# A scan that keeps fourteen state chunks in a ring and reads a whole step out at once

## The reference, cut to what matters

```
h = layernorm(patches of x) @ W + bias, layernorm      # 32 images, 14 x 14 patches -> 196 tokens of 256
h = concatenate([h, txt])                              # 77 text tokens more: 273 tokens
# attention stand-in: every second token goes through a gated recurrence
x_sub = rmsnorm(layernorm(h)[:, ::2]); x, gate = split(x_sub @ w_in.T + b_in)
for each of the 137 steps:                             # state: 32 batches x 256 x 64
    state = tanh(state * A + x_t[:, :, None] * Bm)
    y_t   = state @ c_sum + Dv * x_t
h = h + repeat((y * silu(gate)) @ w_out.T + b_out, 2)
h = h + down(silu(gate(ln(h))) * up(ln(h)))            # integer weights, hidden size 768
```

## Time and profile before

| | |
|---|---|
| median of three runs | 1458.93 us |
| profiled execution | 1453.06 us |
| its span | 1451.3 us |
| PE (matmul) busy | 1244.6 us (86%) |
| DVE busy | 1076.0 us (74%) |
| ACT busy | 1005.0 us (69%) |
| POOL busy | 483.4 us (33%) |
| mean granted TensorE clock | 0.957 of full speed |

### The profile page before, as it was taken

The page is one execution under the profiler, slowest core; times in us unless marked ns, Lnnn a source line. Parts: engine busy times, 40 slices in busy tenths (PEclk is TensorE's granted clock), DMA queues, the critical chain, the costliest instruction groups (busy, mean ns, idle before and its releaser), DMA issues.

```text
span 1451.3 us, 25794 instructions
## 1 busy us (share of the span) xinstructions
PE 1244.6 (86%) x7119; PEld 636.8 (44%) x7119; DVE 1076.0 (74%) x2401; ACT 1005.0 (69%) x1955; POOL 483.4 (33%) x463
## 2 busy tenths in 40 slices
PE   3777889898998989999999999998888989879855
PEld 1642445454544444445445544544344334333333
DVE  4667878787878697878687878776877878768721
ACT  1367686868776868686868786866866867758622
POOL 5213151525343434433334343432222131221231
PEclk9789999999999999999999999999999999999987
DMA  6221414132232314141404050303132231222110
GB/s 180 64 65 32 96 46 96 52 88 72 67 84 55 89 51 102 37 111 28 116 23 120 20 126 13 103 18 101 43 88 75 65 88 50 74 62 63 52 51 7
DMA packets 154925, 100.50 MB, mean 69 GB/s; under 512 B 129088, under 2 KB 143296, under 8 KB 153536
## 3 DMA queue, kind: packets, MB, share of 16 engines
q1 hardware_dynamic: 154880, 99.95, 27.3%
HBM read 58.85 MB, written 41.06 MB: 69 GB/s over the span
## 4 chain that ended last, share of the span: by engine, by line
PE 42%; ACT 21%; issue 11%; DVE 9%; DMA 8%; SPq 4%; POOL 2%; ACTq 1%; DVEq 0%; POOLq 0%
PE P L1179 9%; PE Y L1135 9%; ACT h L883 9%; PE U L1125 8%; DMA raw<-in_x 6%; DVE U L695 5%; PE P L1269 4%; PE P L1270 4%; PE P L1224 3%; ACT rawn L894 2%; PE P L1210 2%; ACT xT_act L967 2%; ACT xT_act L900 2%; ACT fsg L963 2%; ACT y_fx L950 1%
## 5 line engine op out<-in xcount | busy, mean ns | idle before, releaser
L695 DVE TENSOR_TENSOR U<-h,a_col 128x512 f32<-128x512 f32 x1096 | 726.1, 690 | 199.2 <-ACT h L883 193.0
L883 ACT ACTIVATE h<-U 128x512 f32<-128x512 f32 x1096 | 627.2, 601 | 293.1 <-PE U L1125 290.2
L1125 PE MATMUL U<-x_diag,b_st 128*128 128x512 f16 x1096 | 395.7, 392 | 120.7 <-DVE U L695 110.2
L1135 PE MATMUL Y<-h,read_st 128*32 128x512 f32 x2192 | 300.3, 621 | 0.7 <-ACT h L883 0.7
L1125 PEld LDWEIGHTS U<-x_diag,b_st 128*128 128x128 f16 x1096 | 105.8, 100 | 385.4 <-DVE U L695 290.2
L1065 POOL TENSOR_TENSOR xT_act<-act,xT_act 128x448 f16<-128x448 f32 x120 | 123.0, 1038 | 209.3 <-ACT xT_act L967 209.3
L1179 PE MATMUL P<-tok_w,xT_act 128*112 128x256 f32 x672 | 167.8, 385 | 0.9 <-ACT xT_act L900 0.9
L1179 PEld LDWEIGHTS P<-tok_w,xT_act 128*112 128x112 f32 x672 | 118.8, 179 | 40.2 <-issue 11.2
L1284 PE MATMUL P<-down_w,xT_act 128*112 128x256 bf16 x480 | 116.6, 279 | 4.9 <-POOL xT_act L1065 4.9
L1285 PE MATMUL P<-down_w,xT_act 128*112 128x256 bf16 x480 | 115.4, 277 | 0.0
L1019 POOL TENSOR_TENSOR yT<-yT,gate_fx 128x448 f32<-128x448 f32 x20 | 22.7, 1133 | 272.2 <-DMA yT<-y_scr 272.2
(11 more groups left out here) (135 smaller groups left out, 1466.6 us busy)
## 6 DMA issues: line engine op xcount, KB each, us to landing
raw<-in_x SPq DMA_DIRECT2D x42, 448.0 KB, 6.1
tok_scr<-tok SPq DMA_DIRECT2D x20, 448.0 KB, 3.3
gate_scr<-gate_o SPq DMA_DIRECT2D x20, 448.0 KB, 2.5
gate_fx<-gate_scr SPq DMA_DIRECT2D x20, 448.0 KB, 5.0
res<-tok_scr SPq DMA_DIRECT2D x20, 448.0 KB, 3.7
out<-res SPq DMA_DIRECT2D x76, 112.0 KB, 2.3
x_diag<-scan_scr SPq DMA_DIRECT2D x320, 16.0 KB
x_diag<-scan_scr SPq DMA_DIRECT2D x304, 12.0 KB
```

The lines of the kernel that those rows point to most:

```text
L695: dve.tensor_tensor(U[bank_of(slot)][:, :].rearrange("p (l b) -> p l b", b=B), h[:, c, :].rearrange("p (l b) -> p l b", b=B), a_col[:, c * ...
L883: sc.activation(h[:, c, :], U[bank_of(slot)][:, :], ACT.Tanh, scale=1.0 / U_SCALE).then_inc(squashed, 1)
L1125: pe.matmul(U[bank_of(slot)][:, :], b_st[:, c, :], x_diag[:, c, :, t * B:t * B + B], start=False, stop=True, skip_group_check=True).then_i ...
L1135: mm = pe.matmul(Y[c4 * 32:c4 * 32 + 32, :], read_st[:, t, half, :], h[:, half * RG + c4, :], start=(j == 0), stop=(t == steps - 1), skip_ ...
```

## The change

The tile `h` gets 14 places instead of 8 and is used as a ring: slot n writes place n mod 14, and `grow` of slot n reads place (n-8) mod 14. 56 slots are four rounds of the ring, so the numbering goes on through the bodies. The old state of a chunk now lives until 14 slots later. `read_group` becomes `read_step`: eight matmuls for one step, behind the drive of slot 8t+11 (and, for a scan's last step, behind the drive of slot 3 of the next body). On SP the load of yT moves ahead of the text loads. All tables have other numbers. `h` is cleared at the start over its new length; the program is built with a smaller scratch area for software-made DMA descriptors (`dynamic_dma_scratch_size=8192`), and it issues no DMA from POOL.

```diff
-READ_AT = 2
+READ_AT = 3
+RING = 14
...
     "text": dict(
-        ... attend=(13, 17) ... finish=(10, 12) ... ln_stats=(11,), ln_shift=(15,), ... y_copy=(2,)
+        ... attend=(19, 20) ... finish=(15, 17) ... ln_stats=(20,), ln_shift=(21,), ... y_copy=(3,)
...
-        h = sb("h", [128, CHUNKS, CW])
+        h = sb("h", [128, RING, CW])
...
+            if post:
+                sp.wait_ge(y_wr, (q + 1) * 64)
+                sp.sem_inc(passed, 1)
+                for d2 in range(2):
+                    sp.dma_start(yT[d2:127 + d2:2, :, :, :]..., y_scr[:, :, :, d2, :]...).then_inc(y_ld, 16)
             if pre and not image:
...                                                      # the text loads
-            if post:
-                sp.wait_ge(y_wr, (q + 1) * 64)
-                ...                                      # the same two loads of yT
...
-                                  h[:, c, :].rearrange("p (l b) -> p l b", b=B),
+                                  h[:, (slot - CHUNKS) % RING, :].rearrange("p (l b) -> p l b", b=B),
...
-                sc.activation(h[:, c, :], U[bank_of(slot)][:, :], ACT.Tanh, scale=1.0 / U_SCALE)...
+                sc.activation(h[:, slot % RING, :], U[bank_of(slot)][:, :], ACT.Tanh, scale=1.0 / U_SCALE)...
...
-            def read_group(j, s, steps):
-                t, half = divmod(j, 2)
-                pe.wait_ge(squashed, s * SLOTS + (j + 1) * RG)
-                if j == 0 and due(s):
+            def read_step(t, s, steps):
+                pe.wait_ge(squashed, s * SLOTS + (t + 1) * CHUNKS)
+                if t == 0 and due(s):
                     pe.wait_ge(y_out, s)
-                for c4 in range(RG):
-                    mm = pe.matmul(Y[c4 * 32:c4 * 32 + 32, :], read_st[:, t, half, :], h[:, half * RG + c4, :], ...)
+                for half in range(CHUNKS // RG):
+                    for c4 in range(RG):
+                        mm = pe.matmul(Y[c4 * 32:c4 * 32 + 32, :], read_st[:, t, half, :],
+                                       h[:, (t * CHUNKS + half * RG + c4) % RING, :], ...)
...
-                    if slot % RG == READ_AT and slot >= RG:
-                        read_group(slot // RG - 1, s, steps)
+                    if slot % CHUNKS == READ_AT and slot >= CHUNKS:
+                        read_step(slot // CHUNKS - 1, s, steps)
                     elif slot == READ_AT and due(s):
-                        read_group(SLOTS // RG - 1, s - 1, STEPS)
+                        read_step(STEPS - 1, s - 1, STEPS)
```

More of the change, by code:

```diff
@@ L63 @@
     "image": dict(
[L64 to L72, removed]
+        shrink=(0, 0, 0, 2, 5, 5, 6, 7), turn=(9, 9, 10, 11, 15, 15, 16, 16), attend=(17, 18), average=(22, 26),
@@ L77 @@
-        res_stats=(24,), res_variance=(26,), res_shift=(28,), fx_low_part=(35, 35), ln_stats=(11,), ln_shift=(15,),
-        x_low_part=(38,), ffn_product=(40, 44, 45, 49, 53, 55), y_copy=(2,), fx_apply=(27, 27, 28, 29),
-        fxT_copy=(31, 32), ln_apply=(14,), xaT_copy=(17,), x_copy=(24,), gate_silu=(41,), ffn_silu=(36, 38, 40, 46,
-        48, 53), act_high_part=(48, 50, 53, 54, 55, 55)),
+        shrink=(6, 7, 8, 8, 13, 13, 14, 16), attend=(19, 20), turn_fx=(33, 33), ffn_gate=(36, 40, 42, 45, 48, 53),
@@ L81 @@
     "last": dict(
[L82 to L85 removed]
+        shrink=(5, 5, 5, 5, 5, 5, 7, 8), attend=(16, 18), turn_fx=(31, 31), ffn_gate=(34, 35, 35, 48, 53, 54),
@@ L105 @@
     "image": (
[L106 to L110 removed]
+        ("gating", 0), ("residual", 0), ("res_rsqrt", 0), ("raw_rsqrt", 0), ("token_rsqrt", 0), ("token_tiles", 0),
@@ L113 @@
+        ("skip_term", 0), ("act_low_part", 2), ("act_low_part", 3), ("act_low_part", 4), ("act_low_part", 5)),
+    "last": (
+        ("gating", 0), ("residual", 0), ("skip_term", 0), ("res_rsqrt", 0), ("act_low_part", 0),
         ("act_low_part", 1), ("act_low_part", 2), ("act_low_part", 3), ("act_low_part", 4), ("act_low_part", 5)),
-    "last": (
-        ("gating", 0), ("residual", 0), ("res_rsqrt", 0), ("act_low_part", 0), ("act_low_part", 1),
-        ("act_low_part", 2), ("act_low_part", 3), ("skip_term", 0), ("act_low_part", 4), ("act_low_part", 5)),
@@ L880, in squash @@
             def squash(slot):
-                t, c = divmod(slot, CHUNKS)
                 sc.wait_ge(driven, s * SLOTS + slot + 1)
-                sc.activation(h[:, c, :], U[bank_of(slot)][:, :], ACT.Tanh, scale=1.0 / U_SCALE).then_inc(squashed, 1)
+                sc.activation(h[:, slot % RING, :], U[bank_of(slot)][:, :], ACT.Tanh, scale=1.0 / U_SCALE).then_inc(squashed, 1)
             def y_copy():
@@ L1326, in tensor_body @@
                 if scan and steps < STEPS and slot == slots - 1:
-                    read_group(slots // RG - 1, s, steps)
+                    read_step(steps - 1, s, steps)
         IMAGE = dict(image=True, ahead=True, pre=True, scan=True, post=True, down=True, steps=STEPS)
```

83 lines of the change are left out of this document (45 added, 38 removed).

## The result

The changed kernel takes 1426.7 us, the median of four runs (1424.8 to 1428.86); the kernel before took 1460.24 us on the same chip (four runs, 1458.82 to 1468.16). The ratio is 0.976, with a 95% interval of 0.9721 to 0.9798: faster, by 29 to 41 us. The profiled execution took 1426.25 us, its span 1424.4 us, and the mean granted clock was 0.945 of full speed (0.957 before).

A forecast was written before the change was run, and what follows sets the result against it. PE was taken as nearest its limit, though no engine is full all the time. Terms -20 + 4 - 15.5 - 9.6 + 2 = -39 us on 1453.06 give 1414; with 5.9 to the median, 1420 us (1408 to 1432; 80% range 1392 to 1457).

The forecast's parts named there:

- term 1: Read-outs on PE: eight matmuls together save 0.24 us a step; -20 us over image bodies 1 to 13 (0 to -44).
- I count 92%: Image bodies: of 21.8 us PE time saved, 92% counted as gain, because PE is busy for 92% of them.
- Term 2: Copy of Y in image bodies: ACT waits about 2.4 us each, mostly covered; 0.3 us a body, +4 us (0 to +25).
- Term 3: Text bodies 14 to 18: yT earlier, `ln_stats` and `attend` later, both stalls go; 3.1 us a body, -15.5 us (0 to -25).
- the residual chain: Text bodies: attention bias at slot 23, statistics at 28, named as what is late next, with the FFN behind it.
- Term 4: Last text body: its 6.5 us excess goes through SP's new order and later slots; -9.6 us (-3 to -12).
- Term 5: Body 0: POOL's second root goes before the scaling, so everything up to the first drive is later; +2 us (0 to +3).
- At nothing: Items priced at zero: longer clearing of `h`, the tail, and the other moves in the image table.
- the range's far end: Image table's other moves might close the third quarter's gaps, 2.9 us a body, -35 us over 12 bodies.
- Slower: Rival: the long read-out starves DVE and ACT, which wait for tanh; about 1479 us, chance 16%.
- The saved time turns into waiting: Rival: saved PE time becomes waiting for tanh, or each four pays the change-over; about 1440 us, chance 25%.
- The clock holds: Rival: image bodies' third-quarter gaps close and PE stays at 2.4 GHz, 19 us more gained; about 1400 us, chance 17%.

The follow-up runs named there:

- run 3: Changed kernel with each step's read-out split into two fours at slots 8t+11 and 8t+12, a scan's last step whole: 1459.39 us, ratio 0.9978.
- Run 9: Changed kernel with `y_copy` at slot 3 instead of 2 in the image table: 1426.21 us, ratio 0.9754.
- run 12: run 11 with the text bodies' layer norm, its transposes and first two projections later: 1422.55 us, ratio 0.9749.
- run 6: Changed kernel with the text loads ahead of yT on SP again: 1424.71 us, ratio 0.9741.
- run 5: Kernel before with only the load of yT moved ahead of the text loads on SP: 1475.47 us, ratio 1.012.
- Run 8: Changed kernel with body 0's plan and POOL order of before: 1420.61 us, ratio 0.9713.
- run 7: Kernel before with `h` as a ring of 14 places and nothing else: 1457.77 us, ratio 0.9997.
- run 11: Changed kernel with reads in fours, old tables and old SP order in text bodies and tail, and body 0's old plan: 1411.13 us, ratio 0.9658.
- run 1: Changed kernel (ring, merged read-out) with all tables and SP's order of before: 1592.69 us, ratio 1.0906.
- run 2: Changed kernel with reads in two groups of four at slots 4j+6, new tables kept: 1511.59 us, ratio 1.0347.

## Why the prediction was right, and where not

**The total** was right: 1426.7 against a forecast of 1420, within the forecast's own range (1408 to 1432). The mechanism of term 1 was right; that the total fits is luck. Image bodies gained 31 us more than forecast, terms 3 and 4 were 32 us short, and body 0 and the tail cost 11 us more. On the profiled executions that leaves the sum 12 us short, and 5 of these came back because the forecast added 5.9 us from profile to median and the changed kernel's profile lies at its median.

**Term 1, the read-outs: mechanism right, size too small.** The eight take 2.17 us with their drive, to the hundredth. The 0.24 us of change-over is paid once for eight. What failed is "I count 92%": run 3 shows 0.45 us on the path for each 0.26 us of PE time. A drive that is late also delays its tanh and the grow that waits for it, which would explain it; that is argued. For the six change-overs that run 3 puts back, the 13 image bodies lose 31.4 us, where the prediction's way of counting gives 17 (78 x 0.24 x 0.92). The other 16 of the 47 us are not the read-outs': run 3 has them too, 12 by the clock and 4 in body 1. The Trainium skill (TensorEngine Tiling (Array Packing), Key Properties) says that changing the tiling mode drains the engine and changing the tile does not. By both timelines the trace agrees: eight matmuls pay once (2.17 us with the drive), two fours pay twice (1.31 us each with theirs).

**Term 2: right in size of the wait (2.3 us), its price not borne out.** Run 9 takes a third of the wait away in image bodies and gains nothing, where 0.3 us a body was expected. What the rest of the wait costs was not tried.

**Term 3 failed.** The step was to read the excess of quarter 1 over quarter 2, 2.3 us, as what a removed stall returns. Both stalls went, and quarter 1 fell by 3.6 us, but the body did not get shorter. Three things stood behind it.

- *PE's work.* The table clears quarter 1 by moving two blocks of the down projection and one of the output projection into quarter 2, and it moves one block of the input projection and one of the FFN from quarter 3 to quarter 4, where PE was already full (14.1 of 14.1 us). Run 3 shows this without the merged form and at full clock: quarter 1 takes 11.84 us, the others 15.21, 15.35 and 16.62, and the body 59.02 against 58.15 before. The forecast had 2.3 us less; it was 0.9 us more.
- *The next late input.* Where only the layer norm and what uses it move later (run 12), the scan runs into the gated y, which the stall for the text had hidden. The prediction named the residual chain as next.
- *The clock, which the prediction left out of this term.* The merged form takes the body from 59.0 to about 57.0 us (the estimate above), more than the 0.8 us forecast. But bodies 14 to 18 have 34.1 us of half-clock time instead of 3.4, 30.7 us more; at 1.4 us for each 3.4 that is 12.6 us, more than the merged form gave. By this estimate the five bodies come to 0.9 x 5 - 2.0 x 5 + 12.6 = +7 us; measured is +6.4.

**Term 4 failed with it.** SP's order is worth nothing under the new table (run 6) and costs 1.2% under the old (run 5). The wait for the text in the last text body shrank from 7.60 to 3.31 us and quarter 1 from 20.9 to 13.0, but quarters 2 to 4 grew from 15.6, 14.0 and 14.1 to 18.9, 17.4 and 16.0. With reads in fours (run 3) this body takes 62.2 us, 2.5 less than before; the merged form puts 3.0 on it, with 13.7 us of half-clock time instead of 3.4.

**Term 5: right mechanism, a third of its size.** POOL's second root goes first, but it waits for its statistics until 59.83 us, so the scaling starts at 60.49 and not at 58.2, because the embedding ahead of it is later too (DVE takes its last tokens out of PSUM at 57.74 instead of 55.84); `ln_stats` starts at 63.15 instead of 60.8, a half-clock stretch of 13.7 us begins at 60.4 (before: 6.8 us from 60.7), and the first drive is at 86.2. Run 8 gets it back.

**At nothing.** Right for clearing `h` (6.07 us, and POOL still idle for 2.79 before its next task) and for the ring (run 7). Wrong for the tail, +5.5 us: with reads of four and the old tables it is 105.6 (run 11). With the merged reads and all old tables it is 110.1 (run 1), with reads of four and the new tables 109.7 (run 2): either alone costs most of it, and no run shows by what way. And wrong for "the other moves in the image table", in two respects. Without them the merged read-out loses 9% (run 1), so they are the condition of the gain. And with them run 3 gains 16 us in the image bodies, 12 of them by the clock. The third quarter's gaps did close, but not for the 2.9 us a body of the range's far end, since others opened in quarters 2 and 4.

**The rivals.**

*Slower* is refuted for this kernel; the waits for tanh fell. Run 1 shows that it was near: with the old tables the merged read-out costs 135 us, and DVE waits for tanh for 313.0 us.

*The saved time turns into waiting* is refuted by run 3 for the image bodies; in text bodies 14 to 18 it came true in its outcome (298.9 us with the merged form, 299.1 without), but by the lost clock and not by waits for tanh (DVE waits 45.8 us for them in these bodies, 49.4 in run 3).

*The clock holds* came true in the image bodies: 12 us by run 3, where the rival had 19. Before, PE's clock fell in bodies 2 to 13 mostly at slots 10, 11, 36 and 37; in the changed kernel it falls at slot 2, and once at slot 8. The rival's support, that text bodies hold 1.00, did not last: the last one was at 0.95 already, and in the changed kernel all six are under 1.00. The Trainium skill (TensorE: Matmul & The Clock Gate, Part 1) has the gate follow how busy PE has been. Busy shares of whole bodies do not order it here: the text body at 1106.70 before has PE busy for 88% at 1.00, the one at 1125.79 after for 89% at 0.92. The new falls in text bodies stand at slots 2 to 5, in quarter 1, from which the table took PE work, and at slots 32 and 33, in quarter 3, with one more at slot 23 of the last. Run 3, with the same table and two change-overs a step, has 13.7 us of half-clock time there instead of 47.8. Why the merged form loses the clock in text bodies and not in image bodies stays open, and whether a fuller quarter 1 would keep it was not tried.

## What to carry to other kernels

A table of slots and what it places are one thing: the merged read-out under the old tables costs 9%, the new tables with the reads at their old places cost 3.5%, both together gain 2.4%. Change form and place in separate runs: reads in fours at the new places cost nothing against the kernel before (run 3). Before a removed stall is priced at its own length, ask what the stall had hidden and whether the engine that bounds the next stretch has room; a quarter that gets shorter proves nothing until the body does. PE time in front of a drive can cost more than its own length (here 1.8 times). And add the clock up by stretches: PE work that is saved can be lost again to the lower level, as in the text bodies here.

## What the runs showed of the hardware

- Going from full-array matmuls to four column strips and back costs 0.24 to 0.26 us, once for each uninterrupted run of strip matmuls, whether it has four or eight (0.24 is what the 1.31 and 2.17 us leave beside columns and drive, 0.26 is PE's busy time in run 3).
- The same 300 matmuls of a text body ran at a granted clock of 1.00 in one order (58.15 us, before) and of 0.90 to 0.97 in another (58.29 to 65.16 us, after). A half-clock stretch of 3.4 us adds about 1.5 us to an image body (66.17 and 67.73 us above) and about 1.4 us to a text body.
- Fewer change-overs did not always keep the clock: the six text bodies had 13.7 us of half-clock time with two a step (run 3) and 47.8 us with one (the changed kernel).
